# Attention with interleaved filler work: the even chunks' steps three slots later, the odd chunks' sums one body earlier

## The reference

```python
x = x + 0.5 * ffn(layernorm(x))    # linear 512x512 + bias, plus the top 2 of 8 LoRA experts (router, softmax)
x = x + attn(layernorm(x))         # 32 query heads, 8 key/value heads, head size 16
x = x + 0.5 * ffn(layernorm(x))
```

## Time and profile before

| what | value |
|---|---|
| median of 3 runs | 1163.4 us (1157.81 to 1164.84) |
| time of the profiled execution | 1162.77 us |
| its span in the profile | 1161.0 us |
| mean granted TensorE clock, as a share of full | 0.959 |
| TensorE busy | 1061.4 us (91%) |
| VectorE busy | 837.9 us (72%) |
| ScalarE busy | 727.0 us (63%) |
| DMA, share of 16 engines (queue 1) | 18.9% |

### The profile page before, as it was taken

The page is one execution under the profiler, slowest core; times in us unless marked ns, Lnnn a source line. Parts: engine busy times, 40 slices in busy tenths (PEclk is TensorE's granted clock), DMA queues, the critical chain, the costliest instruction groups (busy, mean ns, idle before and its releaser), DMA issues.

```text
span 1161.0 us, 16018 instructions
## 1 busy us (share of the span) xinstructions
PE 1061.4 (91%) x5776; PEld 466.8 (40%) x5776; DVE 837.9 (72%) x1107; ACT 727.0 (63%) x1361; POOL 295.4 (25%) x485
## 2 busy tenths in 40 slices
PE   5989887999999999999999999999999999999647
PEld 4778661344334422333334333433343334233236
DVE  5766679767777777876787778777877887871274
ACT  6556432757865786675676667666767675768311
POOL 5355546302420240410050023003200420041010
PEclk9989886999999999999999999999999999999869
DMA  7122331021211123111211121121113010301300
GB/s 254 46 81 88 100 103 49 27 73 36 60 49 35 33 59 105 31 32 48 87 31 31 61 75 31 31 87 48 31 31 110 30 40 17 115 10 33 108 0 37
DMA packets 70507, 68.31 MB, mean 59 GB/s; under 512 B 15132, under 2 KB 52508, under 8 KB 70428
## 3 DMA queue, kind: packets, MB, share of 16 engines
q1 hardware_dynamic: 70428, 67.29, 18.9%
HBM read 41.95 MB, written 24.63 MB: 57 GB/s over the span
## 4 chain that ended last, share of the span: by engine, by line
PE 72%; DVE 13%; ACT 5%; DMA 3%; issue 3%; POOL 3%; SPq 1%; DVEq 0%; ACTq 0%; POOLq 0%
PE ps_out L1516 19%; PE ps_score L1504 18%; PE ps_max L1485 16%; PE ps_fill L1441 5%; DVE neg_max L1312 5%; ACT probs L1018 2%; PE ps_fill L1470 2%; PE ps_fill L1423 2%; PE ps_fill L1445 1%; DVE neg_max L1110 1%; DVE zd L1184 1%; PE ps_out L1441 1%; PE ps_fill L1409 1%; PE ps_fill L1415 1%; DVE xn L1252 1%
## 5 line engine op out<-in xcount | busy, mean ns | idle before, releaser
L1018 ACT ACTIVATE probs<-ps_score 128x512 f32<-128x512 f32 x992 | 539.0, 597 | 262.0 <-PE ps_score L1504 260.9
L1312 DVE TENSOR_REDUCE neg_max<-ps_max 128x1 f32<-128x1024 f32 x480 | 570.9, 1219 | 179.7 <-PE ps_max L1485 177.7
L1504 PE MATMUL ps_score<-qst,kst 99*128 99x512 bf16 x992 | 308.9, 387 | 10.1 <-ACT probs L1018 8.5
L1485 PE MATMUL ps_max<-kst,qst 96*128 96x512 bf16 x1024 | 290.1, 389 | 16.8 <-DVE neg_max L1110 5.8
L1516 PE MATMUL ps_out<-probs,v_ring 128*32 128x512 f32 x2048 | 274.7, 608 | 7.3 <-ACT o_sb L1027 4.9
L1504 PEld LDWEIGHTS ps_score<-qst,kst 99*128 99x128 bf16 x992 | 76.0, 97 | 273.6 <-ACT probs L1018 232.4
L1485 PEld LDWEIGHTS ps_max<-kst,qst 96*128 96x128 bf16 x1024 | 91.4, 99 | 144.5 <-issue 19.5
L852 POOL CAST shift<-neg_max 128x16 bf16<-128x16 f32 x32 | 9.2, 286 | 435.0 <-DVE neg_max L1312 430.6
L1516 PEld LDWEIGHTS ps_out<-probs,v_ring 128*32 128x32 f32 x2048 | 40.9, 108 | 95.6 <-issue 87.2
L948 ACT ACTIVATE xn<-xc,ln_shift,rstd 128x512 f32<-128x512 f32 x48 | 38.6, 814 | 30.6 <-POOL ln_shift L748 19.6
L1441 PE MATMUL ps_fill<-wb_h,xt_h 128*128 128x512 f32 x84 | 47.1, 561 | 1.0 <-DVE xc L1299 0.8
(11 more groups left out here) (254 smaller groups left out, 1296.6 us busy)
## 6 DMA issues: line engine op xcount, KB each, us to landing
qst<-q_dram SPq DMA_DIRECT2D x192, 64.0 KB, 2.2
att_dram<-o_sb SPq DMA_DIRECT2D x31, 256.0 KB, 2.1
q_dram<-zm SPq DMA_DIRECT2D x24, 256.0 KB, 2.6
kst<-k_dram SPq DMA_DIRECT2D x192, 32.0 KB, 2.2
xc<-x SPq DMA_DIRECT2D x8, 512.0 KB, 4.0
x_dram<-xc SPq DMA_DIRECT2D x8, 512.0 KB, 2.9
xc<-x_dram SPq DMA_DIRECT2D x8, 512.0 KB, 5.6
out<-xc SPq DMA_DIRECT2D x8, 512.0 KB, 3.1
```

The source lines that it names most:

```text
L1018: act.activation(probs[:, kt % 2, j, :], score_bank(i, uu, j), ACT.Exp, scale=1.0 / HD ** 0.5).then_inc(probs_ready, 1)
L1312: dve.tensor_reduce(neg_max[:, uu % 2, t:t + 1], ps_max[max_slot(uu, pos)][:, :, :], AXY, ALU.max, negate=True).then_inc(max_read, 1)
L1485: last = pe.matmul(ps_max[slot][:, half, :], qst[0:SR, r, j, q * P:(q + 1) * P], kst[0:SR, r, half * 512:half * 512 + 512], start=True, st ...
L1504: pe.matmul(score_bank(i, uu, j), kst[0:SR + PARTS, uu, kt * P:(kt + 1) * P], qst[0:SR + PARTS, uu, j, :], start=True, stop=True).then_inc ...
```

## The change

Even back chunks (0, 2, 4) have all their steps six lines (three slots) later. Their lines 59 to 62 thereby fall into lines 1 to 4 of the next body, ahead of that body's odd chunk; line 63 is put on 62. Odd chunks (1, 3, 5) keep their lines, but NR and NL: these move to lines 54 and 57 of the body ahead, and the odd chunk's `load_att` moves to slot 24 of that body. The odd chunk's `load_x1` moves from slot 4 to slot 8, since the chunk ahead of it stores its rows only then. The even chunk's `load_att` and `load_x1` stay at slots 2 and 4. The tail is as it was.

```diff
+LINES = 2 * UB * KT
+EVEN_SHIFT = 6
+EARLY = {"NR": 54, "NL": 57}
...
-        def back_plan(chunk):
-            return {k: [(chunk, step) for step in line] for k, line in enumerate(BACK)}
+        def back_plan(i):
+
+            plan = {}
+            for n in range(max(i - 3, 0), min(i - 1, LOOP_BACKS - 1) + 1):
+                for k, line in enumerate(BACK):
+                    for step in line:
+                        at = LINES * (n + 2) + k + (EVEN_SHIFT if n % 2 == 0 else 0)
+                        if n % 2 == 1 and step in EARLY:
+                            at = LINES * (n + 1) + EARLY[step]
+                        if at // LINES == i:
+                            plan.setdefault(min(at % LINES, LINES - 2), []).append((Chunk("back", 0, n), step))
+            return plan
...
-                    if slot == 2 and load_next is not None:
+                    if slot == 2 and load_next is not None and load_next.n % 2 == 0:
                         if load_next.n > 0:
                             sp.wait_ge(filler_ready[0], Chunk("back", 0, load_next.n - 1).written("T1b"))
                         load_att(load_next)
-                    if slot == 4 and load_next is not None:
+                    if slot == 24 and load_next is not None and load_next.n % 2 == 0:
+                        if load_next.n > 0:
+                            sp.wait_ge(att_low_ready[0], 2 * load_next.n)
+                        load_att(Chunk("back", 0, load_next.n + 1))
+                    if load_next is not None and slot == (8 if load_next.n % 2 else 4):
                         load_x1(load_next, chunk_loaded[0])
```

More of the change, by code:

```diff
@@ L681, in _ @@
                 ch = Chunk("back", 0, i - 2)
-                body(i, back_plan(ch), ch)
+                body(i, back_plan(i), ch)
             ch = Chunk("back", 0, 5)
-            body(7, back_plan(ch), ch, last=True)
+            body(7, back_plan(7), ch, last=True)
             for ch in tail:
@@ L897, in _ @@
             for i in range(2, 7):
-                body(i, back_plan(Chunk("back", 0, i - 2)))
-            body(7, back_plan(Chunk("back", 0, 5)), last=True)
+                body(i, back_plan(i))
+            body(7, back_plan(7), last=True)
             for item in tail_steps():
@@ L1050, in _ @@
             for i in range(2, 7):
-                body(i, back_plan(Chunk("back", 0, i - 2)))
-            body(7, back_plan(Chunk("back", 0, 5)))
+                body(i, back_plan(i))
+            body(7, back_plan(7))
             copy_out(8, -1)
```

## The result

The changed kernel takes 1169.2 us (median of 8 runs, 1164.3 to 1171.2), the kernel before, in 8 runs, 1162.9; the ratio is 1.005, with a 95% interval of 1.0031 to 1.0069. That is 6.2 us more: slower, clearly so by the interval, and by half a per cent. Two executions in all, one of the kernel before (1507.7 us, clock 0.65) and one of an experiment (1819.8 us, clock 0.70), fell into a far slower state and are left out of the medians and ratios here. The profiled execution of the changed kernel took 1170.4 us and its span is 1168.5 us.

What follows compares the result with a forecast made beforehand. TensorE's work was taken to bind, with only waits to gain or lose. Waits removed (-2.44, -1.69), new even-body waits with clock (+6.75) and smaller terms (+0.9, -0.6) gave +2.9: 1163.4 to 1166.3 us, range 1157 to 1171.5.

Steps and rivals of the forecast that it cites:

- a threshold of 1%: About 11.6 us, taken as what a measurement of this kernel can tell from no change.
- What bound the kernel and what could be won: TensorE's work binds; only waits can be won, 2.44 us in body 2 and 1.69 in body 3.
- The odd chunks: Bodies 3, 5, 7: early NR and NL remove body 3's excess, -1.69 us; 0 in bodies 5 and 7.
- The even chunks' trip behind `load_qk`: Bodies 2, 4, 6: reciprocals' store behind 12 issues, N0a 1.0 us late; with the clock 3 x 2.25 = 6.75 us.
- the rate row of body 7: Traffic ending at 1010.5 after issues from 1005.53, taken as 5.0 us for the four reciprocal loads.
- The rule of the Trainium skill: DMA estimate, 2.1 us store and 2.3 us last load: reciprocals at about b+34.0, no wait; supports rival in time, chance 0.24.
- The clock: TensorE partly at 1.2 GHz after idling at N0a: about 1.25 us beyond each wait; rival without this charge, chance 0.10.
- Smaller terms: Even chunks: overhead of `kt` 0 and 1 slots no longer hidden, +0.9 us; moved FFb matmuls covering overhead, -0.6.
- +0.9: Stall moved to slots 11 and 12 can't hide the `kt` 0 and 1 overhead: +0.3 us in each of three bodies.
- -0.6: FFb0 to FFb4 moved into slots 0 to 2 of odd bodies cover overhead there: -0.2 us each.
- The clamp: GpSimd's C1 behind `split_shift` uses up P1's slack of over 4 us; rival: 1 us late in three bodies, 1169.3, chance 0.06.
- The sum: All terms on the profiled execution: -2.44-1.69+6.75+0.9-0.6 = +2.9 us.

Runs made afterwards that it cites:

- the second profile: The changed kernel profiled once more, with nothing changed; that execution took 1172.9 us.
- the even trip early: The changed kernel with NR and NL of the even chunks back at lines 8 and 9; 1160.3 us, ratio 0.997 to the kernel before.
- half a slot later: The kernel before with `load_x1` at slot 8, plus ScalarE's rounding of N0a and N0b one line later; 1153.9 us, ratio 0.9899 to the kernel before.

## Why the prediction came out as it did

The forecast was 1166.3 us, 2.9 more than before, within 1157 to 1171.5, and no change by a threshold of 1%; measured were 1169.2 and 6.2 more. The mechanism was right, the price of the low clock was too small. The threshold was too coarse as well: the interval of the ratio is 0.4% wide, and a loss of 0.5% is clear of it.

*What bound the kernel and what could be won:* right. The waits of bodies 2 and 3 were worth 2.44 and 1.69 us, and the kernel before with `load_x1` at slot 8 got back just these (113.17 and 112.42 to 110.75 and 110.74). Taking apart the time by pairs of bodies shows the same for the shift: 221.5 us with and without it.

*The odd chunks:* right in body 3, -1.7 us, and 0 elsewhere. But the prediction gave the credit to the early NR and NL. The even chunks' shift alone shows body 3 free without them, because `load_x1` at slot 8 was enough; either of the two does it. The rows for this were at hand (4.59 and 3.64 us for a 32 KB store, which the prediction itself places behind the 512 KB of `load_x1`) and were used only as a bound for the store elsewhere.

*The even chunks' trip behind `load_qk`:* right, place and size. Forecast were the store's issue at b+27.67, the reciprocals at b+34.9, N0a ready at b+33.92 and a wait of 1.0 us in each of bodies 2, 4 and 6. Measured in body 4 were b+27.64, b+35.1, b+33.91 and 1.31, with 1.03 and 0.98 in the other two. Within it the store was quicker (1.7 for 2.2) and the four loads slower (5.8 for 5.0), two misses that in part cancelled; that b+34.9 was met so closely is luck to this extent. The loads were as slow as in body 2 before, so the rate row of body 7 was the wrong neighbour, for two reasons that the trace before shows: the row gives the end of the traffic and not the landing, and in body 7 SyncE issued nothing behind the loads until 1013.88, where here the 256 KB of the unit's store followed 1.0 us behind the last. How much each is worth is open. The rule of the Trainium skill (DMA: Bandwidth & Descriptors, Anatomy of one DMA), which the page gives for transfers that GpSimd issues, while SyncE issues these, made the wait vanish and would have been 1.1 us out: its 2.1 us for the store was near the measured 1.7, its 2.3 us for the last load was not near 3.85.

*The clock:* the term that was mis-sized. The prediction took 1.25 us for each wait, 3.75 in all, from stretches of about 3.4 us at the lower clock (2 x 0.15 x 11.21). In the changed kernel the stretches are 6.7 us and cost 111.81-107.76-1.31 = 2.7 us in body 4 and 2.8 in body 6, and nothing in body 2: 5.5 us together; in the second profile 2.5 in each, 7.5. The price of a stretch of 3.4 us was right (1.2 to 1.3 in the kernel before, 1.4 with the even trip early): what the prediction had wrong is its length, twice that in every body of the changed kernel where the clock fell. Why it was twice as long is open. The Trainium skill gives the penalty of such a stretch as its length times the share of clock that is missing (TensorE: Matmul & The Clock Gate, Terms), which makes 3.4 us of 6.7. The traces agree in kind, with 2.5 to 2.8: TensorE's busy time in the slots 11 to 13 is 13.86 us in body 4 and 10.99 in body 2, 2.9 more and not 3.4, so by this estimate it had work for 5.7 of the 6.7 us.

*Smaller terms:* +0.9 and -0.6 were both small, and their sum, +0.3, was 0.1 or less. The clamp came as late as reckoned, without a price. GpSimd in body 4, the split and C1, and VectorE's P1:

```profile
710.80 0.20 POOL L869 CAST shift<-neg_max 128x16 bf16<-128x16 f32 x1 [4.35 <-DVE neg_max L1329]
...
711.94 1.91 POOL L797 TENSOR_SCALAR zd<-zm 128x512 f32<-128x512 f32 x1
...
715.98 0.62 POOL L826 TENSOR_SCALAR zm<-zm 128x512 f32<-128x512 f32 x1
```

```profile
717.24 0.73 DVE L1218 COPY_PREDICATED zm<-zm,zd 128x512 f32<-128x512 int32 x1
```

C1 stands behind the split and ends at 716.60, and P1 starts 0.6 us later without having waited. The slack of over 4 us is down to these 0.6.

*The sum:* +2.9 was forecast. With the clock's 5.5 in place of 3.75, waits of 3.3 for 3.0, and 0.1 for 0.3, it is -4.1+3.3+5.5+0.1 = +4.8, and bodies 2 to 7 did grow from 658.5 to 663.2 us. The profiled executions differ by 7.6 because body 2 also began 1.7 us later (429.99 for 428.31), ahead of the first changed step, and the part behind body 7 took 1.1 us more (75.32 for 74.23), with a granted clock of 0.73 there for 0.77. Neither need be the change's: among the profiles here body 2 begins anywhere from 424.4 to 431.7, and the part behind body 7 takes 73.8 to 75.6, short and long both with and without the shift. The medians differ by 6.2, between the sum with two stretches of low clock and that with three, +7 or so; that the unprofiled runs had two or three is not shown.

## What to carry to other kernels

Count a DMA trip's deadline in the queue that issues it: list what that queue issues ahead of it at the new place, and what is still in flight, before moving consumer and trip together. Moving the trip and its consumer by the same number of slots keeps their distance in the plan and not in time. A step that one engine waits for from another belongs behind the work that the waiting engine could still do; half a slot later was worth 6.2 us here, where the rearrangement with its shift put right (eight lines) was worth 3.9.

## What was not expected of the hardware

- Whether a stall brings the lower clock varies between executions: body 2 of the changed kernel had it in one of two profiles, with waits of 1.03 and 0.9 us, the one without it having the longer wait; body 2 with the even trip early had it with no wait at all. Why is open.
- In bodies 2 to 7 of all ten profiles a stretch at the low clock was 3.4 or 6.8 us long, never between. A long wait cost less beyond itself (0.6 to 1.9 us for 3.4 to 4.3 us) than a short one (2.5 to 2.8 us for 0.9 to 1.3 us), where the clock fell.
- A 32 KB store behind a 512 KB load landed 0.1 to 0.8 us after that load in all of bodies 2 to 7, and so took 4.6 us when issued 1.5 us behind it and 1.6 when issued 3.4 us behind. Without the load it took 2.4 us in body 2, and 1.7 behind twelve loads of 32 and 64 KB.
